# A transformer layer on one core: WO, the first norm and the second norm's end at other places of the step order

## The reference

```
q = rope(x wq + 4 x Aq Bq);  k = rope(x wk);  v = x wv + 4 x Av Bv      # 16 heads of 16
x = layernorm(x + softmax(causal(q k' / 4)) v wo)
h = gelu(butterfly(x W_exp + b_exp) + up_bias)                          # 1024 wide, exact gelu
x = layernorm(x + butterfly(h) W_con + b_con + down_bias)
```

## Time and profile before

| | |
|---|---|
| three runs | 1256.70, 1257.11, 1268.77 us (median 1257.11) |
| profiled execution | 1254.64 us, of it 1252.9 us span |
| mean granted clock | 0.948 of 2.4 GHz |
| busy share | PE 89%, DVE 70%, ACT 54%, POOL 39% |
| instructions | 27672 |

### The profile page before, as it was taken

One profiled execution on the slowest core, in us unless ns is written; L12 is line 12 of the kernel. 1 busy time (PEld: TensorE's weight loads), 2 busy tenths in 40 slices (PEclk: granted clock), 3 DMA queues, 4 the chain that ended last, 5 costly groups with the idle time before them and its releaser, 6 DMA issues.

```text
span 1252.9 us, 27672 instructions
## 1 busy us (share of the span) xinstructions
PE 1112.8 (89%) x8462; PEld 810.3 (65%) x8462; DVE 871.8 (70%) x1951; ACT 673.6 (54%) x1067; POOL 488.1 (39%) x539
## 2 busy tenths in 40 slices
PE   4677699999998989999998989999898999989877
PEld 3444377667676666767666766767666676767565
DVE  6679767676767676776768777676867677676332
ACT  2267566474745647473655647464664747465601
POOL 5334326352442535243352635244253524332310
PEclk9778799999999999999999999999999999999889
DMA  7763445545454565545445564545455455541110
GB/s 253 183 180 105 141 109 163 142 143 146 120 170 116 165 137 158 127 142 148 117 151 132 161 144 138 146 119 160 117 167 144 145 130 141 156 119 55 53 60 17
DMA packets 94983, 169.90 MB, mean 136 GB/s; under 512 B 14872, under 2 KB 36120, under 8 KB 94944
## 3 DMA queue, kind: packets, MB, share of 16 engines
q1 hardware_dynamic: 93888, 166.53, 48.6%
q10 hardware_dynamic: 832, 1.83, 0.4%
q0 software_dynamic: 224, 1.04, 0.2%
HBM read 92.28 MB, written 77.07 MB: 135 GB/s over the span
## 4 chain that ended last, share of the span: by engine, by line
PE 56%; DVE 17%; issue 10%; DMA 7%; ACT 4%; POOL 2%; SPq 2%; DVEq 0%; ACTq 0%; POOLq 0%
PE ps_m L550 18%; PE ps_m L699 13%; PE ps_m L669 8%; PE ps_m L598 5%; DVE m_raw L895 4%; PE ps_t L641 4%; DMA m_scr<-m_row 3%; PE ps_m L678 3%; DVE stats L949 2%; PE ps_m L684 2%; DVE y L964 2%; DMA q_st<-m_scr 2%; DVE m_raw L890 2%; PE ps_m L627 2%; ACT pT L771 1%
## 5 line engine op out<-in xcount | busy, mean ns | idle before, releaser
L771 ACT ACTIVATE pT<-ps_t 128x512 f32<-128x512 f32 x640 | 330.4, 602 | 232.6 <-PE ps_t L641 231.0
L895 DVE TENSOR_REDUCE m_raw<-ps_m 128x1 f32<-128x512 f32 (+2 forms) x768 | 338.3, 504 | 98.7 <-PE ps_m L627 95.0
L1036 POOL TENSOR_SCALAR_AFFINE_SELECT pT<-pT 128x512 f32<-128x512 f32 (+1 forms) x320 | 174.8, 553 | 393.5 <-ACT pT L771 393.5
L699 PE MATMUL ps_m<-w,gact 128*128 128x256 f32 x1024 | 235.3, 384 | 1.1 <-ACT gact L841 1.1
L699 PEld LDWEIGHTS ps_m<-w,gact 128*128 128x128 f32 x1024 | 190.7, 190 | 29.7 <-ACT gact L841 1.5
L598 PE MATMUL ps_m<-k_st,q_st 48*128 48x512 f32 (+3 forms) x1024 | 152.4, 353 | 42.7 <-DVE rope_in L914 18.2
L669 PE MATMUL ps_m<-pT,v_aug 128*32 128x512 f32 (+3 forms) x2048 | 156.2, 447 | 2.0 <-POOL pT L1036 1.4
L598 PEld LDWEIGHTS ps_m<-k_st,q_st 48*128 48x128 f32 x1024 | 88.8, 190 | 102.8 <-issue 87.1
L641 PE MATMUL ps_t<-q_st,k_st 50*128 50x512 f32 (+3 forms) x1024 | 128.3, 354 | 7.4 <-DMA q_st<-m_scr 5.6
L669 PEld LDWEIGHTS ps_m<-pT,v_aug 128*32 128x32 f32 x2048 | 58.5, 112 | 86.1 <-issue 79.5
L942 DVE TENSOR_TENSOR y<-ps_m,y 128x256 f32<-128x256 f32 x64 | 27.2, 425 | 121.7 <-PE ps_m L699 121.7
(11 more groups left out here) (106 smaller groups left out, 1678.9 us busy)
## 6 DMA issues: line engine op xcount, KB each, us to landing
qk_scr<-rot_hi SPq DMA_DIRECT2D x64, 512.0 KB, 3.6
q_st<-qk_scr SPq DMA_DIRECT2D x128, 192.0 KB, 4.7
k_st<-qk_scr SPq DMA_DIRECT2D x128, 192.0 KB, 5.1
qk_scr<-rot SPq DMA_DIRECT2D x32, 512.0 KB, 3.2
o_scr<-o_raw SPq DMA_DIRECT2D x64, 256.0 KB, 3.6
r_b<-in_xT SPq DMA_DIRECT2D x17, 512.0 KB, 7.4
o_c<-o_scr SPq DMA_DIRECT2D x32, 256.0 KB
r_b<-r_scr SPq DMA_DIRECT2D x32, 256.0 KB
```

The lines of the kernel that those rows point to most:

```text
L699: mm = pe.matmul(pm[:, 0:D], gact[:, k, n * P:(n + 1) * P], w2[:, k, :], start=(k == 0), stop=(k == NHT - 1))
L771: act.activation(pT[:, g % 2, slot, half * T:(half + 1) * T], ps_t[:, ST_BANK[2 * n + r], :], ACT.Exp, scale=SCALE).then_inc(exp_done, 1)
L895: ins = dve.tensor_reduce(m_raw[:, r, u // 2, qt:qt + 1], scores[:, off:off + (qt + 1) * P], AX.X, ALU.max, negate=True)
L1036: pool.affine_select(out=v, in_=v, compare_op=ALU.is_ge, fill=0.0, base=0, pattern=pattern, channel_multiplier=-1).then_inc(mask_done, 1)
```

## The change

`early` and `late` change their lists, and two new places are added to a phase: `between(p)`, behind the STs and before the second S, and `last(p)`, behind the SELs.

- W2 tile 2 goes from phase 4 to phase 3, tile 3 from phase 5 to phase 4.
- Phase 5 has both WO tiles, with the first half's statistics between them; the second half's follow the scores, and the first norm's aggregation ends the phase. The normalisation of x_res stands in phase 6 between the two score steps. The transposes XT of phase 7 stand behind V instead of ahead of it.
- Of the second norm, LNS 3 goes from phase 5 to 6, LNA from 6 to the end of 8, LNB and OUT from 7 to 9.
- BIAS goes from the head of phase 0 to its end, XRES from the head of phase 1 to its `late`.

```diff
         if p == 0:
             put("FILL", i, 3)
-            put("BIAS", i - 2, 0)
-            put("BIAS", i - 2, 1)
...
         elif p == 1:
-            put("XRES", i - 1, 0)
-            put("XRES", i - 1, 1)
...
             gemm("W2", i - 2, 1)
+            gemm("W2", i - 2, 2)
         elif p == 4:
             put("QKL", i + 1, 1)
-            gemm("W2", i - 2, 2)
+            gemm("W2", i - 2, 3)
...
         elif p == 5:
-            gemm("W2", i - 2, 3)
             gemm("WO", i - 1, 0)
+            put("LNS", i - 1, 0)
+            gemm("WO", i - 1, 1)
             put("FILL", i + 1, 1)
         elif p == 6:
-            gemm("WO", i - 1, 1)
-            put("LNS", i - 1, 1)
-            put("LNA", i - 1, 0)
             if not static or i >= 0:
                 gemm("V", i + 1, 0)
             gemm("MT", i, 3)
-            put("LNB", i - 1, 0)
-            put("LNB", i - 1, 1)
             gemm("PV", i, 1)
         elif p == 7:
+            if not static or i >= 0:
+                gemm("V", i + 1, 1)
             gemm("XT", i - 1, 0)
             gemm("XT", i - 1, 1)
-            if not static or i >= 0:
-                gemm("V", i + 1, 1)
...
+    def between(p):
+
+        if p == 6:
+            put("LNB", i - 1, 0)
+            put("LNB", i - 1, 1)
+
     def late(p):
...
+        elif p == 1:
+            put("XRES", i - 1, 0)
+            put("XRES", i - 1, 1)
...
         elif p == 5:
+            put("LNS", i - 1, 1)
             put("XTL", i + 2, 0, B + 1)
+        elif p == 6:
             put("LNS", i - 2, 3)
-            put("LNS", i - 1, 0)
-        elif p == 6:
-            put("LNA", i - 2, 1)
             put("MROW", i, 3)
             put("RAW", i, 1)
         elif p == 7:
-            put("LNB", i - 2, 2)
-            put("LNB", i - 2, 3)
             put("SMOC", i, 0)
             put("XHI", i + 2, 0, B + 1)
             put("FILL", i + 1, 2)
-            put("OUT", i - 2)
...
         elif p == 9:
             put("RAW", i, 2)
+            put("LNB", i - 2, 2)
+            put("LNB", i - 2, 3)
+            put("OUT", i - 2)
+
+    def last(p):
+
+        if p == 0:
+            put("BIAS", i - 2, 0)
+            put("BIAS", i - 2, 1)
+        elif p == 5:
+            put("LNA", i - 1, 0)
+        elif p == 8:
+            put("LNA", i - 2, 1)
+        elif p == 9:
+            put("ON", i, 0)
...
         put("ST", i, t + 1)
+        between(p)
         put(*ahead[1])
         late(p)
         put("SEL", i, t)
         put("SEL", i, t + 1)
-        if p == NU // 2 - 1:
-            put("ON", i, 0)
+        last(p)
```

## The result

The changed kernel takes 1316.14 us in the median (1309.0 to 1316.5, four runs) against 1257.61: 1.043 times the kernel before (95% interval 1.036 to 1.050). The forecast was 1310, the range 1277 to 1325. The profiled execution has a span of 1314.7 us where the one of before had 1252.9.

What follows compares the result with a forecast made beforehand. TensorE, busy 89%, was taken to set the loop's pace. Terms +3.2 (WO), +1.7 (clock), 0 (WO to W1), -1.4 (W1), +0.2 (phase 9) gave +3.7 us a period, +55.5 over 15 batches: 1310 us, range 1277 to 1325.

Steps and rivals of the forecast that it cites:

- WO's wait: Before WO: RCP starts later against PE, which loses one W2 tile of cover; PE waits 3.2 us in each batch.
- The clock behind it: Behind WO's wait: half clock for 3.4 us of WO tiles, losing 1.7 us a batch, bounds 0 and 2.6.
- rival C: More is lost: half clock twice as long, or x_res's normalisation held up by GpSimd; 1324 us, chance 0.17.
- WO to W1: From WO's start to the first W1 tile: 17.6 to 18.0 us, DVE's list binding; change 0, within 0.4.
- W1: Before the fourth W1 tile: the wait of 1.36 us goes, counted as -1.4 us a batch.
- Phase 9: Second norm's four steps on y, moved here beside the selections: 0.2 us lost, bounds 0 and 0.8.
- A: Behind WO the clock stays up: +2.0 us a batch, 1285 us, chance 0.17.
- B: Faster: WO's wait replaces other waits and the clock is up behind it; -0.9 us a batch, 1241 us, chance 0.06.
- D: The change doesn't move RCP, so no WO wait or clock loss: -1.2 us a batch, 1237 us, chance 0.03.

Runs made afterwards that it cites:

- W2 alone: The kernel before with only W2 tile 2 moved to phase 3 and tile 3 to phase 4: 1326.17 us, 1.053 times before.
- W2 back: The changed kernel with W2 tile 2 back in phase 4 and tile 3 back in phase 5: 1230.94 us, 0.977 of the kernel before.
- RCP early: The changed kernel with RCP, REC and RB of phase 3 put between its two W2 tiles: 1223.96 us, 0.972 of the kernel before.
- filler: The changed kernel with W2 tile 3 computed twice, useless work ahead of WO: 1287.52 us.
- second norm alone: The kernel before with only LNS 3, LNA 1, LNB 2 and 3, OUT, BIAS and XRES at their new places: 1218.08 us, 0.967.
- LNS 3 late: RCP early with LNS 3 moved from phase 6 to phase 7, behind the maxima: 1216.17 us, 0.966 of the kernel before.
- LNS 3 kept: The second norm alone with LNS 3 back in phase 5, ahead of LNS 0: 1234.42 us, 0.981 of the kernel before.

## Why the prediction was right

*WO's wait*: 3.2 us forecast, 3.10 measured, ended by ON, with RCP 8.38 us before ON's end (8.3 forecast). Shown as the W2 lines' doing by W2 alone and W2 back, and as RCP's place by RCP early.

*The clock behind it*: the mechanism was right, the term too small. I took 1.7 us from a spell of 3.4; it lasts 6.9, and the filler puts its price at 2.7. That is rival C's first half, and just above the 2.6 that I gave as the upper bound. The row of batch 0 had shown it: PE busy 5.58 us at a clock of 0.50, 2.8 us lost by half. I took that row's wait but not its spell.

*WO to W1*: 17.6 to 18.0 at full clock were forecast. Measured are 20.17, less the 2.7, so 17.5; W2 back and RCP early, at full clock, have 17.45 and 17.55 in their periods. MT waits 0.92 (0.9 forecast). That the first norm's own part wins nothing but the clock is shown by the kernel that has it alone. The forecast of 0 was against a stretch that held XT's wait and LNS 3; against the second norm alone, whose stretch is 16.5 us, the new order is the longer one.

*W1*: the 1.36 us are gone, as forecast. *Phase 9*: the four steps on y take 2.01 where 1.38 would do, beside two selections, but PE shows no wait from it, so 0 for 0.2. What was not in the sum: the rest of the period, from W1 0 to WO less its wait, fell by (71.68 - 17.86) - (75.01 - 20.17 - 3.10) = 2.1 us, of which W1 explains 1.4; the wait in phase 1 is 0.84 in place of about 1.0, and the remaining half microsecond isn't taken apart. This and the clock's 1.0 are opposite errors: +3.3 a period measured, +3.7 forecast. The total (+59, forecast +55) is near by a further accident. At 3.3 a period it would have been 50; the rest was lost mostly in the first three whole periods, which the sum took to be like the others: from XT to XT they grew from 68.1, 70.6 and 70.8 us to 77.4, 75.2 and 75.1. The first of them ran at 1.00 before and at 0.93 after. So the mechanism was foreseen, and the nearness of the number is in part luck.

*Blind spot*: I counted LNS 3 at its new place, in DVE's list, but gave its leaving the old one no term of its own. In the second norm alone that counts 0.65 us a batch and more through the clock. In the changed kernel it stands behind the second score instead, where taking it out is worth 0.5 us (RCP early against LNS 3 late), so the total hid the omission.

*Rivals*: A and B would need the clock at 1.00 behind WO, and it is 0.51. D falls by RCP's time: PE comes to WO 5.3 us behind RCP in place of 8.8. Of C the second half failed: the normalisation of x_res in its new place took 1.56 us against 1.38, a loss of 0.2 where I had allowed 1.0. The Trainium skill ("SBUF — State Buffer", "Who interferes with whom") calls the port pair that VectorE shares with GpSimd an exclusive lock. The 2.01 us of the steps on y beside two selections and these 1.56 agree with it in that both are above 1.38; the loss beside such short instructions is small.

## What to carry to other kernels

When work is moved ahead in an order that all engines share, look for the short steps of other engines that now stand behind it: here a 0.53 us reciprocal, first link of an 8.3 us chain through DRAM, lost its cover of one W2 tile. Price an idle stretch of TensorE with the clock that follows it; here a wait of 3.1 us cost 5.8. And test a change by its parts and by their pairs: the second norm's part won 40 us by itself, the first norm's 6, both together only 27, and the W2 lines lost 68 by themselves and 85 with the others.

## What was unexpected of the hardware

The same wait of 1.9 us before XT was followed by half clock in one period and not in the next, with periods of 70.7 and 69.2 us alternating through most of the loop (LNS 3 kept). An average price for such a wait doesn't hold for a single period. And useless matmuls in place of a wait made the kernel 28.6 us faster.
